# Attention with two accumulator sets in turn, outputs copied out raw, and the division moved into the next chunk

## The reference

```python
q, k, v = split(layer_norm(t) @ W_qkv)              # 4 heads of 32
q, k = l2norm_axis1(q), l2norm_axis1(k)
attn = softmax(einsum('bihd,bjhd->bhij', q, k) * 10.0, axis=-1)
out = einsum('bhij,bjhd->bhid', attn, v)            # then @ W_out + b_out
```

## Time and profile before

| | us |
|---|---|
| median of three runs | 5882.98 |
| the profiled execution, its own time | 5884.61 |
| its span | 5882.9 |
| TensorE busy, matmuls | 4708.2 (80%) |
| VectorE busy | 5070.9 (86%) |
| ScalarE busy | 3751.1 (64%) |
| GpSimd busy | 1666.3 (28%) |

### The profile page before, as it was taken

The page is one execution under the profiler, slowest core; times in us unless marked ns, Lnnn a source line. Parts: engine busy times, 40 slices in busy tenths (PEclk is TensorE's granted clock), DMA queues, the critical chain, the costliest instruction groups (busy, mean ns, idle before and its releaser), DMA issues. The chain is left out here.

```text
span 5882.9 us, 100771 instructions
## 1 busy us (share of the span) xinstructions
PE 4708.2 (80%) x33880; PEld 1953.7 (33%) x33880; DVE 5070.9 (86%) x6502; ACT 3751.1 (64%) x4897; POOL 1666.3 (28%) x1274
## 2 busy tenths in 40 slices
PE   5776779998777777999867777799986677779997
PEld 3222433333322243333332224333343222433334
DVE  6799779998689977999878997799987899679998
ACT  3666468883466646888346663688924666378882
POOL 1488600000048860000004885000000588500000
PEclk9899989999889998999988999899988899989998
DMA  1000020000000002000000000200000000020000
GB/s 38 0 1 0 15 62 9 9 5 22 22 0 1 0 15 62 9 9 5 22 22 0 1 0 15 62 9 9 5 22 22 0 1 0 15 62 9 9 5 15
DMA packets 41626, 87.14 MB, mean 15 GB/s; under 512 B 11672, under 2 KB 27872, under 8 KB 38112
## 3 DMA queue, kind: packets, MB, share of 16 engines
q1 hardware_dynamic: 41184, 81.11, 5.2%
HBM read 26.55 MB, written 8.39 MB: 6 GB/s over the span
## 5 line engine op out<-in xcount | busy, mean ns | idle before, releaser
L1296 ACT ACTIVATE arena<-ps 128x1024 f32<-128x1024 f32 x2048 | 1912.8, 1027 | 258.9 <-PE ps L1261 241.3
L1311 DVE TENSOR_TENSOR arena<-arena 128x1024 f32<-128x1024 f32 x1664 | 1907.8, 1218 | 35.9 <-ACT arena L1296 30.6
L941 DVE TENSOR_TENSOR_SCAN arena<-ps,hlast,arena 128x512 f32<-128x512 f32 x1024 | 1259.4, 1266 | 5.2 <-DVE arena L923 3.2
L901 POOL TENSOR_TENSOR arena<-arena 128x1024 f32<-128x1024 f32 x512 | 1206.8, 2357 | 25.0 <-issue 2.1
L1261 PE MATMUL ps<-arena 128*32 128x512 f16 x16384 | 1093.4, 383 | 118.2 <-issue 47.2
L1244 PE MATMUL ps<-arena 128*32 128x512 f32 x8192 | 1087.4, 609 | 46.0 <-DVE arena L1316 38.1
L870 ACT ACTIVATE ps<-arena,amat 128x512 f32<-128x512 f32 x1024 | 691.9, 688 | 505.1 <-DVE arena L941 504.3
L838 PE MATMUL ps<-arena,ident 128*128 128x512 f32 x2048 | 980.3, 602 | 7.7 <-POOL arena L901 7.7
L1261 PEld LDWEIGHTS ps<-arena 128*32 128x32 f16 x16384 | 470.7, 97 | 975.3 <-issue 650.9
L1619 POOL MEMSET arena<- 128x1024 f32 x4 | 3.8, 956 | 2694.4 <-POOLq L101 2694.4
L923 DVE TENSOR_TENSOR arena<-arena,ps 128x1024 f32<-128x1024 f32 x512 | 611.2, 1194 | 53.8 <-PE ps L846 53.8
(11 more groups left out here) (245 smaller groups left out, 4387.5 us busy)
## 6 DMA issues: line engine op xcount, KB each, us to landing
arena<-x SPq DMA_DIRECT2D x32, 512.0 KB, 5.4
arena<-arena SPq DMA_DIRECT2D x64, 256.0 KB, 6.0
arena<-arena SPq DMA_DIRECT2D x64, 224.0 KB, 5.8
arena<-arena SPq DMA_DIRECT2D x28, 512.0 KB, 3.5
arena<-pe SPq DMA_DIRECT2D x256, 32.0 KB, 1.8
out<-arena SPq DMA_DIRECT2D x8, 1024.0 KB, 3.9
expw<-L_ffn_expert_w SPq DMA_DIRECT2D x1, 512.0 KB
wqkv<-L_attn_W_qkv SPq DMA_DIRECT2D x1, 192.0 KB
```

The source lines that it names most:

```text
L901: pool.tensor_tensor(halves(g[s % 4]), halves(hb[s % 4]), cs[s % 4].unsqueeze(1).broadcast_to([128, HD, CH]), ALU.mult).then_inc(hc_s, 1)
L941: dve.tensor_tensor_scan(halves(hb[s % 4])[:, h, :], da(s, h), halves(dbx[s % 2])[:, h, :], k.hlast[:, s, h, :], ALU.mult, ALU.add).then_i ...
L1296: act.activation(probs[p % 8], k.bank(2 * group[p], 2 * CH), ACT.Exp, scale=SCALE / SPLIT ** 2).then_inc(exp_s, 1)
L1311: dve.tensor_tensor(acc[p % 2], acc[p % 2], probs[p % 8], ALU.add).then_inc(acc_s, 1)
```

## The change

There are two sets of accumulators, used by even and odd chunks. The second lies where the high halves of the queries were staged. ScalarE copies bank O as it is into the output's place (`keep_output`) after exp(2) of the next chunk. VectorE's reciprocal and multiplication (`divide`) come after add(5) of the next chunk; the multiplication reads and writes the output's place in SBUF. TensorE's `finish` moves from after S(2) to after S(4). W(0) now waits for ScalarE's copy, and the first direct sum (block 5) waits for the reciprocal, since it overwrites bank LS. ScalarE's program gets chunk 0 outside its loop; VectorE's gets the shape of TensorE's, with two chunks in the loop's body.

```diff
-    acc = [k.at(SUM_AT + i * 2 * CH, 2 * CH) for i in range(2)]
+    sums = [[k.at(at + i * 2 * CH, 2 * CH) for i in range(2)] for at in (SUM_AT, QH_AT)]
...
-            if j == 0:
-                pe.wait_ge(norm_s, c + 1)
+            if j == 0 and not first(c):
+                pe.wait_ge(o_s, c)
+            if j == direct[0] and not first(c):
+                pe.wait_ge(l_s, c)
...
-        def finish(c):
+        def finish(c, q):
             pe.wait_ge(acc_s, summed(c, NPAIR - 1))
-            ones_by(acc, False, True).then_inc(l_mm, 1)
+            ones_by(sums[q], False, True).then_inc(l_mm, 1)
...
-                    if p == 2 and not first:
-                        finish(c - 1)
+                    if p == 4 and not first(c):
+                        finish(c - 1, 1 - q)
...
     def scalar(act):
+        def keep_output(c):
+            act.wait_ge(pv_s, c * NJ + (NJ + 4))
+            act.activation(ao[:, cols_of(c)], k.bank(O), ACT.Copy).then_inc(o_s, 1)
...
                 act.activation(probs[p % 8], k.bank(2 * group[p], 2 * CH), ACT.Exp, scale=SCALE / SPLIT ** 2).then_inc(exp_s, 1)
+                if p == 2 and not first(c):
+                    keep_output(c - 1)
+        body(0)
+        with act.Fori(1, NCH) as c:
+            body(c)
+        keep_output(NCH - 1)
...
     def vector(dve):
-        with dve.Fori(0, NCH) as c:
+        def divide(c):
+            dve.wait_ge(l_mm, c + 1)
+            dve.reciprocal(rl, k.bank(LS)).then_inc(l_s, 1)
+            dve.wait_ge(l_s, c + 1)
+            dve.wait_ge(o_s, c + 1)
+            dve.tensor_tensor(ao[:, cols_of(c)], ao[:, cols_of(c)], rl, ALU.mult).then_inc(norm_s, 1)
+        def body(c, q):
+            acc = sums[q]
             for p in range(NPAIR):
...
-            dve.wait_ge(l_mm, c + 1)
-            dve.reciprocal(rl, k.bank(LS)).then_inc(l_s, 1)
-            dve.wait_ge(l_s, c + 1)
-            dve.wait_ge(pv_s, c * NJ + (NJ + 4))
-            dve.tensor_tensor(ao[:, bass.ds(c * CH, CH)], k.bank(O), rl, ALU.mult).then_inc(norm_s, 1)
+                if p == 5 and not first(c):
+                    divide(c - 1)
+        body(0, 0)
+        with dve.Fori(0, NCH // 2 - 1) as cc:
+            body(cc * 2 + 1, 1)
+            body(cc * 2 + 2, 0)
+        body(NCH - 1, 1)
+        divide(NCH - 1)
```

More of the change, by code:

```diff
@@ L1210, in attend @@
     probs = [k.at(8192 + i * 2 * CH, 2 * CH) for i in range(8)]
-    acc = [k.at(SUM_AT + i * 2 * CH, 2 * CH) for i in range(2)]
+    sums = [[k.at(at + i * 2 * CH, 2 * CH) for i in range(2)] for at in (SUM_AT, QH_AT)]
     rl = k.at(RL_AT, CH)
     NJ, NPAIR = L // 128, 2 * (L // 128)
-    s_mm, exp_s, pv_s, acc_s, l_mm, l_s, norm_s = (k.sem(n) for n in (
-        "scores_mm", "probs_ready", "pv_mm", "probs_summed", "sums_mm", "sums_inverse", "chunk_normed"))
+    s_mm, exp_s, pv_s, acc_s, l_mm, l_s, o_s, norm_s = (k.sem(n) for n in (
+        "scores_mm", "probs_ready", "pv_mm", "probs_summed", "sums_mm", "sums_inverse", "output_kept", "chunk_normed"))
     O, LS = 6, 7
@@ L1222, in attend, with first @@
     NA = NPAIR - 2 * len(direct)
+    def first(c):
+        return isinstance(c, int) and c == 0
     def summed(c, p):
@@ L1247, in weigh, with body @@
             last.then_inc(pv_s, 1)
-        def finish(c):
+        def finish(c, q):
             pe.wait_ge(acc_s, summed(c, NPAIR - 1))
-            ones_by(acc, False, True).then_inc(l_mm, 1)
-        def body(c, queries, first):
+            ones_by(sums[q], False, True).then_inc(l_mm, 1)
+        def body(c, q, queries):
             for j in range(NJ):
@@ L1264, in body @@
                     last.then_inc(s_mm, 1)
-                    if p == 1 and not first:
+                    if p == 1 and not first(c):
                         weigh(c - 1, NJ - 1)
-                    if p == 2 and not first:
-                        finish(c - 1)
+                    if p == 4 and not first(c):
+                        finish(c - 1, 1 - q)
                 if j in (3, 4):
@@ L1277, in staged @@
             pe.wait_ge(staged_s[i], n * 16)
-            body(c, q_now[i], False)
-        body(0, qs[:, :, 0:CH], True)
+            body(c, i, q_now[i])
+        body(0, 0, qs[:, :, 0:CH])
         with pe.Fori(0, NCH // 2 - 1) as cc:
@@ L1285, in tensor, with body @@
         weigh(NCH - 1, NJ - 1)
-        finish(NCH - 1)
+        finish(NCH - 1, (NCH - 1) % 2)
     def scalar(act):
-        act.sem_inc(exp_s, 3)
-        k.ready_table(act, ACT.Exp, 1)
-        with act.Fori(0, NCH) as c:
+        def keep_output(c):
+            act.wait_ge(pv_s, c * NJ + (NJ + 4))
+            act.activation(ao[:, cols_of(c)], k.bank(O), ACT.Copy).then_inc(o_s, 1)
+        def body(c):
             for p in range(NPAIR):
@@ L1296, in scalar @@
                 act.activation(probs[p % 8], k.bank(2 * group[p], 2 * CH), ACT.Exp, scale=SCALE / SPLIT ** 2).then_inc(exp_s, 1)
-    def vector(dve):
-        dve.sem_inc(pv_s, 4)
-        dve.sem_inc(acc_s, NA)
-        dve.sem_inc(norm_s, 1)
-        with dve.Fori(0, NCH) as c:
+                if p == 2 and not first(c):
+                    keep_output(c - 1)
+        act.sem_inc(exp_s, 3)
+        k.ready_table(act, ACT.Exp, 1)
+        body(0)
+        with act.Fori(1, NCH) as c:
+            body(c)
+        keep_output(NCH - 1)
+    def vector(dve):
+        def divide(c):
[6 more added lines that the diff above has]
+            acc = sums[q]
             for p in range(NPAIR):
@@ L1311, in vector @@
                     dve.tensor_tensor(acc[p % 2], acc[p % 2], probs[p % 8], ALU.add).then_inc(acc_s, 1)
-            dve.wait_ge(l_mm, c + 1)
-            dve.reciprocal(rl, k.bank(LS)).then_inc(l_s, 1)
-            dve.wait_ge(l_s, c + 1)
-            dve.wait_ge(pv_s, c * NJ + (NJ + 4))
-            dve.tensor_tensor(ao[:, bass.ds(c * CH, CH)], k.bank(O), rl, ALU.mult).then_inc(norm_s, 1)
+                if p == 5 and not first(c):
+                    divide(c - 1)
+        dve.sem_inc(pv_s, 4)
+        dve.sem_inc(acc_s, NA)
+        body(0, 0)
[4 more added lines that the diff above has]
+        divide(NCH - 1)
     return tensor, scalar, vector
```

## The result

The changed kernel takes 5823.85 us, the median of four runs (5819.58 to 5826.48), against 5879.81 us of the kernel before on the same chip (5876.56 to 5884.37): a ratio of 0.9902 with a 95% interval of 0.9887 to 0.9918. It is faster by 56 us. Two more comparisons of the same two kernels, on other occasions, gave 0.9919 [0.9902, 0.9935] and 0.9918 [0.9904, 0.9932], with medians of 5829.6 and 5827.89 us. The forecast was 5832 us in a range from 5824 to 5856.

What follows compares the result with a forecast made beforehand. TensorE and ScalarE set the pace inside chunks, with the loss at boundaries where W(0) waits for VectorE's division. 33.7 us of waiting plus 18.3 us of slow clock, 52 us off 5884.6, gave 5832; range 5824 to 5856, own range 5825 to 5840.

Steps and rivals of the forecast that it cites:

- The wait of W(0): At chunk boundaries W(0) no longer waits for the division: 1.26 us at 20, 1.06 us at 8 turning ones, 33.7 us.
- The slow clock: TensorE at 1.2 GHz after idling before W(0): all 11 long stalls before exp(8) go, 11 x 1.66 = 18.3 us.
- Sum: Gain from W(0)'s wait and the slow clock over all boundaries: 33.7 + 18.3 = 52 us.
- VectorE at cost 0: Division after add(5) delays no exponential, 1.3 us to spare at exp(17); 46 adds after it end at 949.6: cost 0.
- Ends at 0: A batch's last chunk divides as before, with a copy beside the reciprocal: cost 0.
- The slow clock that stays: Rival: TensorE's slow stretches remain, gain 33.7 us plus up to half of 18.3, time 5842 to 5851; chance 0.18.
- a late VectorE: Rival: VectorE late for exp(17)'s buffers or at its loop's turn, 1 us lost at each of 28 boundaries, 5860; chance 0.08.
- a change that moves nothing: Rival: the copy waits behind something or the stall reappears before exp(10); time 5883, within noise; chance 0.03.
- the copy reloading tables: Rival: ScalarE loads tables twice per chunk around the copy, 72 us in all, 20 us slower, 5903; chance 0.03.
- The gap at VectorE's turn: VectorE's two-chunk loop might stall like TensorE's at each turn: free if covered, uncovered 8 x 2.2 = 17.6 us, 5850.

Runs made afterwards that it cites:

- both experiments: Kernel before, idle TensorE filled with extra matmuls of S(8): 5869.55 us; changed kernel, W(0) also waiting for exp(6): 5878.49 us.
- order changed: Changed kernel with TensorE issuing the next S between ones-sums and W in direct blocks, and the first W spread out: 5796.91 us, ratio 0.9861.

## Why the prediction was right in its mechanism and missed its range

*The wait of W(0): right.* W(0) was foreseen at 890.65, exp(8) at 893.2, the reciprocal at 893.0; they stand at 890.75, 893.27 and 892.87. A boundary is 10.45 us at all 20 ordinary places (10.5 foreseen). At the turns 1.06 us were foreseen; without the slow clock they take 12.34 us in the mean of four, before 13.67 in the mean of six, 1.33 less. The experiment that held W(0) back took all of it away again.

*The slow clock: right in its cause.* No ordinary boundary has it any more, and both experiments show that it hangs on the idle time ahead of W(0). Its size was taken as a constant, 11 x 1.66, though it is 11 in one execution and 7 in another of the same program. At the turns, where the prediction let it be, it came more often (4 of 8 for 2 of 8), which gives some 3 us back.

*Sum: right for the profiled pair, by terms that cancel.* 52.0 us were measured in the attentions, 52 foreseen. The boundaries give 52.6. Not foreseen were ScalarE's straight chunk 0 (2.4 us less from each first exponential to exp(62), over four batches), and 3.0 us more in the later chunks. These 3.0 us stand at one place, exp(30), which comes 0.07 to 0.3 us later after exp(29) in each of the 28 chunks of ScalarE's loop. The same twelve exponentials, exp(26) to exp(37) of chunk 1, before and after:

```profile
913.48 11.14 ACT L1296 ACTIVATE arena<-ps 128x1024 f32<-128x1024 f32 x12 [0.76 <-PE ps L1261]
```

```profile
912.29 3.78 ACT L1303 ACTIVATE arena<-ps 128x1024 f32<-128x1024 f32 x4 [0.76 <-PE ps L1266]
916.24 7.46 ACT L1303 ACTIVATE arena<-ps 128x1024 f32<-128x1024 f32 x8 [0.17 <-PE ps L1266]
```

VectorE is not the cause: the last add that exp(30) needs is over 3.1 to 3.3 us earlier, and the kernel with the reciprocal twice, where VectorE is 1.5 us later, has the delay in the same size. TensorE's matmuls there have the same spacing as before. All eight traces of the changed kernel and its variants with TensorE's old order have the delay, none of the four traces without the copy has it. The cause stays open.

*VectorE at cost 0: right, on a wrong count.* The prediction had 46 adds after the division; there are 52 adds in a chunk (1664 / 32), four of them ahead of the division, so 48. With 48 the work ends at 951.7 and not at 949.6, as the row of 54.76 us shows, and the chunk's slack is 1 us, not more. It held: from exp(14) on, each add that an exponential needs is over at least 1.5 us before it starts, the least at exp(17), where 1.3 us were foreseen.

*Ends at 0: not quite.* From the last exp(62) to the output projection it is 12.20 us, before it was 12.51: 1.2 us less over four batches. The experiment with one set shows that much more would be lost there without the second set.

*What failed is the last step, from the 52 us to a time*, "So 5884.6 - 52 = 5832.6 for an execution like the profiled one, and I say 5832", and with it the range's lower edge, "the forecast's own range is 5825 (the two slow stretches that also occur at turning boundaries go, and the median has fewer)". Three things went wrong there. The sum starts from one execution that lay high: the kernel before has a median of 5879.81 beside this result, 4.8 us under the 5884.6, and 5879.81 - 52 = 5827.8 lies within the range. The reason given for the lower edge did not hold: the slow stretches at the turns did not go, they came at 4 places instead of 2. And the scatter of executions was put at nothing: 15 executions of the changed kernel lie between 5817.69 and 5836.76 us, wider than the 7 us allowed below the forecast. By medians the gain was 56.0, 46.4 and 51.9 us in the three comparisons, around the 52 of the sum, so that the first of them fell under the edge by 0.15 us is in part chance, as a hit would have been.

In the profiled pair the attention stretch moved as forecast, and outside it the execution after was 8.0 us shorter, 1.2 of them at the batches' ends. For the other 6.8 I have no cause. Without the ends, everything outside the attentions took 3671.5 and 3665.5 us in two executions of the kernel before, 3664.7, 3660.4 and 3656.7 in three of the changed kernel, and 3665.4 to 3670.7 in five variants of it (W(0) held back, finish early, loop written out, order changed, both). Those carry the copy and the second set and don't have the shorter rest, which speaks against a cause in the change. The time that TensorE spent there at 1.2 GHz falls in the same order in the first five (629, 627, 607, 601 and 582 us), but the variants don't all follow it, and no run says which of the two drives the other. It stays open.

*The rivals.* The slow clock that stays, a late VectorE, and a change that moves nothing are out by the rows above. Of the copy reloading tables there is nothing: 32 copies, all between 591 and 617 ns, with no table load at their line:

```profile
L1296 ACT ACTIVATE arena<-ps x32: 591/593/617, 887.8 to 5692.8; 128x512 f32 x28, 128x512 f32<-128x512 f32 x4
```

*The gap at VectorE's turn.* It didn't come, and it was not merely covered. Where TensorE's loop is written out and VectorE's still turns, after chunk 2, VectorE goes from its last add to the copies without idle time:

```profile
1011.27 5.77 DVE L1332 TENSOR_TENSOR arena<-arena 128x1024 f32<-128x1024 f32 x5
1016.95 1.29 DVE L1329 COPY arena<-arena 128x1024 f32<-128x1024 f32 x2
```

The Trainium skill ("Runtime: NRT & Kernel Launch", Instruction fetch mechanics) has the stall only where the target of the jump has left the instruction memory, which it gives as 2048 instructions for TensorE and 512 for most engines. TensorE's two chunks are 2 x (816 matmuls + 816 weight loads) = 3264, VectorE's 2 x 56 = 112, some 330 with their waits in the trace; so by the rule TensorE stalls and VectorE doesn't. The traces agree (2.2 us and none). The prediction used the rule without its size. That the 2.2 us are such a fetch is inferred; what the run with the loop written out shows is that they come with the jump.

## What to carry to other kernels

Where a wait leaves TensorE idle for a microsecond or two, count what the clock does after it as well: here 1.3 us of waiting had another 1.66 us behind it at 3 to 11 of 20 places, and filling the idle time with useless matmuls removed the second part alone. A division that follows an accumulation can be moved off the path by copying the raw result out of the bank, and most of that gain comes from the copy; what the second set of accumulators buys lies mainly at the end of each batch. When a sum of terms is exact, the time still depends on the execution that it is taken from, and the range has to hold the spread of executions; the counts on which a "cost 0" rests (here 48, not 46) are worth counting twice.

## What I had not expected of the hardware

- The granted clock fell after idles of only 1.2 to 2.2 us, and not always: in the same program at 11 or 7 of 20 like places, never at a batch's first boundary, and at 1 to 6 of 8 turns. With the idle filled, at 0 of 20.
- An exponential after a direct block starts 0.62 us after its predecessor's end in ScalarE's straight chunk and 0.76 us in its loop, with the same work on TensorE. The only difference in the program is whether the waits' values are constants or come from the loop's register.
- A jump back over TensorE's two chunks costs 2.2 us with nothing issued; over VectorE's two chunks no gap is seen.
- With a copy after exp(2) in ScalarE's loop, exp(30) starts 0.07 to 0.3 us late in each of 28 chunks, though its scores and the add that it needs are there. No trace says why.
